# The first turn of the two token stages: loading by tile, four banks, a later weight split, copies from a second queue

## The reference

```python
x = x + attention0(norm(x), ctx)      # 16 heads of 32, 154 keys a batch
x = x + experts(norm(x))              # 32 experts, top 8, capacity 512
x = x + attention1(norm(x), ctx)
x = x + light_ffn(x) + heavy_ffn(of 512 routed tokens a batch)

def attention(query, ctx):            # one layer
    q = query @ Wq.T + bq; k = ctx @ Wk.T + bk; v = ctx @ Wv.T + bv
    scores = (q @ k.T * tau + delta) / sqrt(32)
    return softmax(scores) @ v @ Wo.T + bo
```

## Time and profile before

| | us |
|---|---|
| median of 3 runs | 3654.71 (3654.07 to 3657.95) |
| the profiled execution, its own time | 3648.97 |
| its span, first to last instruction | 3647.1 |
| mean granted clock | 0.952 |

### The profile page before, as it was taken

The page is one execution under the profiler, slowest core; times in us unless marked ns, Lnnn a source line. Parts: engine busy times, 40 slices in busy tenths (PEclk is TensorE's granted clock), DMA queues, the critical chain, the costliest instruction groups (busy, mean ns, idle before and its releaser), DMA issues. The chain is left out here.

```text
span 3647.1 us, 55254 instructions
## 1 busy us (share of the span) xinstructions
PE 3293.3 (90%) x16960; PEld 2529.1 (69%) x16960; DVE 2789.6 (76%) x5546; ACT 1549.5 (42%) x5369; POOL 1957.5 (54%) x1819
## 2 busy tenths in 40 slices
PE   5899999999859999999997799999999678878898
PEld 3677777777537777777775577677777466657776
DVE  3788888888677887788774689899898688756675
ACT  0666666666421111111111577777677443211110
POOL 1555555556455666666664566666666433223332
PEclk8899999999979999999998899999999889989999
DMA  6345455454375666666665345455465366411100
GB/s 193 88 134 168 116 146 155 120 153 122 116 207 141 158 166 162 160 157 166 164 159 115 109 136 144 138 165 146 118 172 141 99 223 248 162 47 24 24 12 12
DMA packets 284692, 491.09 MB, mean 135 GB/s; under 512 B 53922, under 2 KB 74722, under 8 KB 283682
## 3 DMA queue, kind: packets, MB, share of 16 engines
q1 hardware_dynamic: 243986, 409.40, 36.9%
q0 software_dynamic: 32256, 77.65, 11.2%
q10 hardware_dynamic: 8208, 1.05, 0.2%
HBM read 250.32 MB, written 136.96 MB: 106 GB/s over the span
## 5 line engine op out<-in xcount | busy, mean ns | idle before, releaser
L835 ACT ACTIVATE t_pr<-ps,t_negmax 128x154 f32<-128x154 f32 x2048 | 869.5, 552 | 365.3 <-DVE t_negmax L617 365.0
L549 POOL TENSOR_TENSOR t_pr<-t_pr,t_inv 128x616 f32<-128x616 f32 x512 | 640.0, 1250 | 576.0 <-DVE t_inv L632 573.0
L835 ACT ACTIVATION_READ_ACCUMULATOR t_pr<-ps,t_negmax 128x1 f32 x2048 | 482.9, 236 | 0.0
L640 DVE COPY t_pTm<-ps 128x512 f32<-128x512 f32 x512 | 350.0, 684 | 164.9 <-PE ps L905 164.2
L617 DVE TENSOR_REDUCE t_negmax<-ps 128x4 f32<-128x616 f32 x512 | 403.7, 788 | 60.3 <-PE ps L892 59.5
L904 PEld LDWEIGHTS ps<-ident,t_pr 128*128 128x128 f32 x2048 | 316.4, 206 | 133.8 <-issue 76.3
L892 PE MATMUL ps<-t_kst,t_stack 98*128 98x154 f32 x2048 | 356.8, 294 | 58.0 <-issue 35.6
L904 PE MATMUL ps<-ident,t_pr 128*128 128x128 f32 x2048 | 343.5, 291 | 19.1 <-DVE t_pTm L640 10.1
L892 PEld LDWEIGHTS ps<-t_kst,t_stack 98*128 98x128 f32 x2048 | 282.9, 196 | 73.1 <-issue 57.7
L74 PE MATMUL ps<-e_xT_high,e_wgu_high 128*128 128x512 f32 x768 | 306.5, 399 | 1.6 <-DVE e_xT_low L1396 1.6
L76 PE MATMUL ps<-e_xT_high,e_wgu_low 128*128 128x512 f32 x768 | 304.9, 397 | 0.0
(11 more groups left out here) (336 smaller groups left out, 8319.6 us busy)
## 6 DMA issues: line engine op xcount, KB each, us to landing
t_stack<-t_q_high SPq DMA_DIRECT2D x1024, 64.0 KB, 2.0
c_wgu_in<-in_gate_upT SPq DMA_DIRECT2D x32, 1536.0 KB, 12.5
t_stack<-t_q_low SPq DMA_DIRECT2D x512, 64.0 KB, 2.0
x_dram<-t_xs SPq DMA_DIRECT2D x32, 1024.0 KB, 6.1
c_wd_in<-in_downT SPq DMA_DIRECT2D x32, 768.0 KB, 13.9
xs_dram<-t_z SPq DMA_DIRECT2D x16, 1032.0 KB, 7.7
l_z<-xs_dram SPq DMA_DIRECT2D x16, 1032.0 KB
t_x<-in_x SPq DMA_DIRECT2D x16, 1024.0 KB
```

The lines of the kernel that those rows point to most:

```text
L549: pool.tensor_tensor(p, p, inv[:, v, :].unsqueeze(1).to_broadcast([P, KEYS, HG]), ALU.mult).then_inc(s["normed"], 1)
L640: dve.tensor_copy(pTm[:, g % 2, :, t * P:(t + 1) * P], ps[:, 4, :].rearrange("p (h n) -> p h n", h=HG)).then_inc(s["pTm"], 1)
L835: op = act.activation(pr[:, u % 4, :, h], flat[:, col:col + KEYS], ACT.Exp, bias=negmax[:, u, h:h + 1], accum_out=total[:, u, h:h + 1])
```

## The change

Eight edits, all for group 0 of each token stage:

1. SP loads x of group 0 with four DMAs, one for each tile, each with a semaphore of its own; VectorE waits for each before that tile's statistics. `x_in` counts from the second group on.
2. The four chunks of group 0's transposes go to banks 3, 0, 1 and 2; the wait for the low part of the chunk before goes away where the bank is not `T_BANK`.
3. POOL waits for all four normalised tiles before it splits the query weights.
4. TensorE runs 90 transposes of the identity into bank 3 ahead of everything in turn -1; nothing reads them and they wait for nothing.
5. Of the 8 high copies of the first `stack_up`, SP issues four, for the first four rows of heads.
6. ScalarE issues the other four, between the first and the second bias step (L770); it waits there for VectorE's rounding.
7. VectorE rounds the second query product of group 0 at the end of turn -1, not behind the first maximum of turn 0.
8. The helper functions take the bank as an argument.

```diff
@@ -67,6 +67,12 @@
 
 
     return engine.tensor_copy(out, src)
+
+
+def keep_running(pe, c, bank, n):
+
+    for _ in range(n):
+        pe.transpose(c["ps"][:, bank, 0:P], c["ident"][:], c["ident"][:])
 
 
 def product(pe, out, left, right, start, stop):
@@ -309,7 +315,7 @@
             ssq, rn, score = sb("ssq", [P, TG]), sb("rn", [P, TG]), sb("score", [P, TG])
         ps = c["ps"]
         s = Sems(nc, ctx, f"t{l}",
-                 "... x_in ..."
+                 "... x_first0 x_first1 x_first2 x_first3 x_in ..."
                  "q_mm q_out q_high q_low scored negmax shared exped inv normed p_mm pTm pTt pv oT_high oT_out proj resid "
                  "s_stats s_mv s_ve s_rstd xl z z_mm zT_dve zT_act side_mm side_out top "
@@ -317,6 +323,8 @@
         block = ctx.enter_context(nc.Block())
         W_IN = 16 * 3
         T_BANK, A_BANK, B_BANK = 3, 6, 7
+        FILL = 90
+        FIRST = (T_BANK, 0, 1, 2)
         APART, BASE, SHARED = 170, (2, 854), (3, 0)
         flat = ps[:].rearrange("p b n -> p (b n)")
         STACK = 16 * 3 * HG
@@ -373,6 +381,10 @@
             for n in range(-1, NG + 2):
                 body(n, n % 2, 0 <= n - 2 < NG, 0 <= n - 1 < NG, 0 <= n < NG, n + 1 < NG, n + 2 < NG, (n - 1) // PER, n // PER)
 
+        def x_bank(j, k):
+
+            return FIRST[k] if isinstance(j, int) and j == 0 else T_BANK
+
         def o_slot(par, k):
 
             return 2 * par + k if k < 2 else 2 + k
@@ -393,7 +405,8 @@
 
         @block.sync
         def _(sp):
-            sp.dma_start(x[:], rows(x_in, 0)).then_inc(s["x_in"], 16)
+            for t in range(TG):
+                sp.dma_start(x[:, t, :], rows(x_in, 0)[:, t, :]).then_inc(s[f"x_first{t}"], 16)
             sp.dma_start(xs[:], a[f"WqT{l}"].rearrange("(k p) n -> p k n", p=P)).then_inc(s["wq_in"], 16)
             with nc.allow_non_contiguous_dma(reason="biases by partition"):
                 sp.dma_start(bq[:], a[f"bq{l}"].rearrange("(k p) -> p k", p=P)).then_inc(s["w_in"], 16)
@@ -411,7 +424,7 @@
             def stack_up(j, n):
 
                 sp.wait_ge(s["q_high"], DC * j + n + 1)
-                for at in (0, 2 * DK):
+                for at in (0, 2 * DK) if (j, n) != (0, 0) else (0,):
                     for h in range(HG):
                         sp.dma_start(stack[at:at + DK, HG * (n % 2) + h, :].bitcast(F32),
                                      qhigh[h * DK:(h + 1) * DK, n % 2, :].bitcast(F32)).then_inc(s[f"stacked{n}"], 16)
@@ -552,6 +565,7 @@
             def turn(i, par, prev2, prev, cur, nxt, nxt2, before, batch):
                 if isinstance(i, int) and i == -1:
                     rstd_of(0, "x", 0)
+                    pool.wait_ge(s["xn"], TG)
                     for k in range(DC):
                         pool.wait_ge(s["wq_high"], k + 1)
                         weight_low(wq, xs, k, "wq_low")
@@ -650,7 +664,7 @@
 
             def x_low(j, k):
                 dve.wait_ge(s["xnT_high"], DC * j + k + 1)
-                dve.tensor_tensor(xnT[1][:, k, :], ps[:, T_BANK, :], xnT[0][:, k, :].bitcast(F32),
+                dve.tensor_tensor(xnT[1][:, k, :], ps[:, x_bank(j, k), :], xnT[0][:, k, :].bitcast(F32),
                                   ALU.subtract).then_inc(s["xnT_low"], 1)
 
             def o_low(i, par, g):
@@ -720,15 +734,19 @@
                         z_turned(j, 2 * ZD.index(at))
                     if at == QH[0] and nxt:
                         query_high(i + 1, 0)
-                    if at in QH[1:] and cur:
+                        if not cur:
+                            query_high(0, 1)
+                    if at in QH[1:] and cur and (i, at) != (0, QH[1]):
                         query_high(i, QH.index(at))
                     if at == LOG and gate and prev2:
                         logits(j)
                     if nxt:
-                        if at == SX[0]:
-                            dve.wait_ge(s["x_in"], 16 * (i + 2))
+                        if at == SX[0] and cur:
+                            dve.wait_ge(s["x_in"], 16 * (i + 1))
                         for t in range(TG):
                             if at == SX[t]:
+                                if not cur:
+                                    dve.wait_ge(s[f"x_first{t}"], 16)
                                 statistics(0, "x", i + 1, x, (t,))
                         for t in range(TG):
                             if at == NX[t]:
@@ -784,7 +802,7 @@
             def x_turned(j, k):
                 act.wait_ge(s["xnT_mm"], DC * j + k + 1)
                 reached(act, s["q_mm"], DC * j)
-                act.copy(xnT[0][:, k, :], ps[:, T_BANK, :]).then_inc(s["xnT_high"], 1)
+                act.copy(xnT[0][:, k, :], ps[:, x_bank(j, k), :]).then_inc(s["xnT_high"], 1)
 
             def z_turned(j, k):
                 act.wait_ge(s["z_mm"], DC * j + k + 1)
@@ -849,6 +867,11 @@
                         if not cur:
                             act.wait_ge(s["w_in"], W_IN)
                         query_out(i + 1, 0)
+                        if not cur:
+                            act.wait_ge(s["q_high"], 1)
+                            for h in range(HG):
+                                act.dma_start(stack[2 * DK:3 * DK, h, :].bitcast(F32),
+                                              qhigh[h * DK:(h + 1) * DK, 0, :].bitcast(F32)).then_inc(s["stacked0"], 16)
                     if at in QO[1:] and cur:
                         query_out(i, QO.index(at))
                     if at in XT and nxt:
@@ -872,9 +895,9 @@
         def _(pe):
             ident = c["ident"]
 
-            def transposes(src, k, done):
+            def transposes(src, k, done, bank=T_BANK):
                 for t in range(TG):
-                    mm = pe.transpose(ps[:, T_BANK, t * P:(t + 1) * P], src[:, t, k * P:(k + 1) * P], ident[:])
+                    mm = pe.transpose(ps[:, bank, t * P:(t + 1) * P], src[:, t, k * P:(k + 1) * P], ident[:])
                 mm.then_inc(done, 1)
 
             def scores(i, u, batch):
@@ -962,9 +985,9 @@
                     pe.wait_ge(s["xn"], TG * (j + 1))
                 if k == 0 and prev2 and gate:
                     pe.wait_ge(s["zT_dve"], 2 * (j - 2))
-                else:
+                elif x_bank(j, k) == T_BANK:
                     reached(pe, s["xnT_low"], DC * j + k)
-                transposes(x, k, s["xnT_mm"])
+                transposes(x, k, s["xnT_mm"], x_bank(j, k))
 
             def z_turn(j, k, cur, nxt):
                 if k == 0:
@@ -997,6 +1020,8 @@
                 mm.then_inc(s["side_mm"], 1)
 
             def turn(i, par, prev2, prev, cur, nxt, nxt2, before, batch):
+                if isinstance(i, int) and i == -1:
+                    keep_running(pe, c, T_BANK, FILL)
                 if isinstance(i, int) and i == 0:
                     pe.wait_ge(s["w_in"], W_IN)
                     pe.wait_ge(s["ones"], 1)
```

More of the change, by code:

```diff
@@ L311, in token_phase @@
         s = Sems(nc, ctx, f"t{l}",
-                 "w_in wq_in wo_in wq_high wq_low wo_high wo_low k_in0 k_in1 k_in2 k_in3 v_in0 v_in1 v_in2 v_in3 x_in xbo_in ready ones x_stored z_stored "
+                 "w_in wq_in wo_in wq_high wq_low wo_high wo_low k_in0 k_in1 k_in2 k_in3 v_in0 v_in1 v_in2 v_in3 x_first0 x_first1 x_first2 x_first3 x_in xbo_in ready ones x_stored z_stored "
                  "stacked0 stacked1 stacked2 stacked3 x_stats x_mv x_ve x_rstd xn xbo xnT_mm xnT_high xnT_low "
```

## The result

| | us |
|---|---|
| before, median of 4 | 3654.39 (3653.73 to 3657.95) |
| after, median of 4 | 3626.85 (3617.41 to 3632.46) |
| ratio | 0.992, 95% interval 0.9898 to 0.9942 |
| the profiled execution after, its own time and span | 3632.46, 3630.4 |

The forecast was 3630, range 3622 to 3642. The change gains 27.5 us by the medians and 16.7 by the two profiled spans. The executions of the changed kernel lie 15 us apart, so the steps have to be read from marks inside the trace.

The account below looks back on a forecast made before the run. TensorE, 90% busy, sits idle at both stage starts, where each us saved counts once a stage. Bias steps 9.1 + 10.4 plus copies 2 x 2.7 = 24.9 us off 3654.7 gives 3630, range 3622 to 3642.

Parts of the forecast that it names:

- The chain up to the split: Start of stage 0: statistics end at 58.8, normalising at 62.8, POOL's split of the query weights at 68.0 us.
- the load by tile: Group 0's x in four DMAs: statistics end 1.8 us earlier, bounds 1.3 later to 1.9 earlier.
- POOL's new wait: POOL splits weights only after normalising, so four normalising steps take 2.1 us instead of 5.70.
- The fill: 90 transposes ahead of turn -1 raise TensorE's clock after about 5 us and end at 65.4, bounds 62.9 to 73.5.
- rival B: Filling transposes never raise TensorE's clock; a stage gains 2.1 us, total 3650.5, no visible change; chance 0.07.
- Rival E: Filling transposes wait for each other, writing the same 128 columns; stage 14.5 us later, total 3684; chance 0.04.
- The bias step: After the first query product: 72.6 instead of 81.67 in stage 0 (9.1 us), 2013.2 instead of 2023.57 in stage 1 (10.4).
- the cover of SP's three extra issues: About 1.3 us of extra issues counted at nothing, absorbed by the first value load's 1.63 us issue.
- The copies: Eight high copies on SP's and ScalarE's queues: gain 2.7 us a stage, bounds 0 and 2.7.
- Rival C: Two queues share what limits an issue, so four copies take as long as eight; 5.4 us lost, 3635; chance 0.12.
- Rival D: Half the gain is given back in turn 0 to a wait that does not move with the start; 3642; chance 0.07.
- The early rounding: VectorE's second query rounding at the end of turn -1: counted at nothing, at most 0.4 us gained.

Follow-up runs that it names:

- e11: Changed kernel with x of group 0 loaded by one DMA again instead of four; 3627.74 us, one run.
- e3: Changed kernel with POOL splitting the query weights at once, without waiting for the normalised tiles; 3624.14 us, ratio 0.9914 to before.
- e1: The changed kernel run again with no edit; median 3632.67 us, ratio 0.9935 to before.
- e10: Changed kernel with 180 filling transposes instead of 90; 3640.08 us, ratio 0.996 to before.
- e4: Changed kernel with all eight high copies of the first stack issued by SP, none by ScalarE; 3628.57 us, ratio 0.9924 to before.
- e12: Changed kernel with VectorE's second rounding back behind the first maximum of turn 0; 3625.81 us, one run.

## Why the prediction was right, point by point

**The chain up to the split: right.** Statistics were to end at 58.8 and did at 58.5, normalising at 62.8 and did at 62.4, the split at 68.0 and did at 67.4. By e11 and e3 it is the load by tile and the later landing of the weights that hold this, and hardly POOL's new wait, to which the prediction gave the shortening from 5.70 to 1.92 us. In stage 1 the split ended at 16.3 us and not at 15.5, as the weights came late.

**The fill: right, and rival B falls.** It was to end at 65.4, its last transpose began at 64.1, and the clock was at 1.00 from 56.8. What the forecast did not count is that the clock can go again in the idle time behind the three chunks, as in e1's stage 1. The Trainium skill's rule that transposes do not count (TensorE: Matmul & The Clock Gate, section Part 4: PE-mode transpose) is not what this chip showed, now for transposes alone. Rival E falls too: all 180 of e10 write the same 128 columns, and the last 90 start 0.111 us apart, no more than the 0.118 of transposes into different ones.

**The bias step: right in stage 0, mis-sized in stage 1.** In stage 0 it was to wait for the gate weights at 72.6 and did at 72.72. That it came so near is partly luck: their load was issued 0.5 us earlier than counted (65.67 against 66.18) and took 7.0 us to land and not 6.4. In stage 1 the forecast had the product last, for a bias step 19.0 us after the start of the stage, and the routing vector in at 18.2. It came at 21.4 and 21.3. In the first trace the vector was last, issued at 14.7 instead of 11.8 and 6.7 us on its way; the product alone would have let the bias step begin at 20.2. In e1 the product was last, at half clock.

The step that failed is the cover of SP's three extra issues, which were put at nothing. The cover, the long issue of the first value load, did shrink in stage 0, from 1.63 to 0.72 us, and the gate weights were issued no later. But it stands behind the query weights in SP's program and could not cover those: they were issued 1.4 us later after the start of the stage, and landed 0.5 us later in stage 0 and 1.9 in stage 1 (not at all and 0.9 in e1). And in stage 1 no such cover had been read: that issue took 0.65 us before and 0.61 after, and the routing vector's issue came 2.9 us later (1.6 in e1).

**The copies: right, a little large.** 2.7 us a stage were counted; the distance from bias step to scores fell from 10.7 and 10.3 to 8.1 and 8.0, 2.6 and 2.3, and e4 gives 2.2. Rival C falls by it.

**Rival D, half of the gain given back in turn 0: not so.** SP's next loads of x, before and after:

```profile
126.09 0.39 SPq L435 DMA_DIRECT2D t_x<-in_x  x1
```

```profile
115.23 0.39 SPq L448 DMA_DIRECT2D t_x<-in_x  x1
```

That is 10.9 us apart, and the two loads after it 12.8 and 13.8 (in e1 11.8, 13.8 and 14.7), against 11.5 at the scores (12.4 in e1). In stage 1 it was 20.6 at the scores and 20.1 and 21.3 at the two loads behind. So at most 0.6 us were given back in turns 0 and 1, not half, but the distance was not constant either: by the last load of stage 0 it was 11.3, and 10.2 at the start of stage 1.

**The early rounding: worth nothing**, as counted (e12).

**The sum.** 24.9 us were forecast. The scores' distance from the stage's start fell by 11.4 and 10.3 us in the first trace and 12.0 and 10.4 in the second, 21.7 and 22.4 in all, against 11.8 and 13.1 forecast. The missing 2.7 are stage 1's: 2.4 at the bias step, by `w_in` in the one trace and by the product's clock in the other, and 0.4 at the copies. The medians gave 27.5 and 19.2, which lie around that, so that the first came within 3 us of the forecast is partly luck. The parts taken away one at a time add up to less than the whole: 1.1 to 1.7 and 0.7 for the fill, 2.2 and 2.2 for the copies, 2.2 to 2.8 and 2.2 for the banks, about 2.9 and 1.6 for the load by tile, nothing for the rounding and for POOL's wait. They hide behind each other, as the chain goes on from whichever of tiles, split, product and loads is last.

**What stays open.** At the start of stage 1's scores the profiled execution was 20.6 us ahead of before (2033.90 against 2013.35), and at the end 16.7. In e1 it was 23.9 and 16.2, and in each of the other eleven traces the distance to this one trace of before was smaller at the end too, by 0.4 to 10.5 us. Nothing in the program differs there. The trace of before is of an execution 5.4 us below its median, which may be a part of it. The same stretch of a later phase, 20 us apart, had this in the trace of before:

```profile
3040.00:3140.00 100.00, 83.67 (x360) 62.40 (x359) 81.60 (x185) 24.44 (x41) 29.91 (x23) 0.91 0.55 202
```

after:

```profile
3020.00:3120.00 100.00, 82.49 (x347) 61.06 (x346) 80.12 (x179) 23.66 (x41) 31.01 (x24) 0.90 0.56 206
```

and in e1:

```profile
3020.00:3120.00 100.00, 83.92 (x347) 62.10 (x346) 79.86 (x180) 23.34 (x40) 29.82 (x23) 0.88 0.55 202
```

TensorE got a lower clock (0.90 and 0.88 against 0.91) and did 347 matmuls where it had done 360. This is one stretch, chosen among many. That where the half-clock stretches fall makes the spread of 15 us, or the loss behind stage 1's start, was only argued.

## What to carry to other kernels

Work out a shortened start as a chain of last arrivals and write down for each link what comes second, the landing of small late loads too: here each edit was worth 1 to 3 us by itself, and in one trace of the second stage a load of 256 KB, issued last, set the end. A cover (here an issue that was slow anyway) has to be read in every place where the change acts, and it covers only what stands behind it. Work that is to raise the clock has to reach near the work that needs it: in e1's stage 1 the idle time between them took most of the gain back. Where executions differ by 15 us and an edit is worth 2, compare marks inside the traces.

## What was not expected of the hardware

- Transposes alone brought TensorE from 0.50 to 1.00 within 4.6 us, as forecast; that the idle time after the fill would cost the clock again was not. In the changed kernel's first trace the product's twelve matmuls took 2.9 us from first to last start in both stages; in e1's stage 1 (3.05 us idle before the fourth chunk) and in e11's stage 0 (3.49 us) they took 4.2, at a granted clock of 0.55 for most of it and of 0.64.
- VectorE's rounding of 128x512 lasted 0.92 and 1.91 us instead of 0.43 while POOL's memset ran, and 0.43 once it was moved.
- SP and ScalarE issued four DMAs each side by side in 2.82 and 2.52 us, against 2.53 for four when SP alone issued (half of e4's 5.06).
- The landing of the same 1 MB load, issued behind the same loads of x, differed by up to 3.8 us between traces (8.6 in e1, 12.4 in e12).
